# A gated attention and feed-forward stack on one core: GpSimd's large dequantisation operations each in four column pieces

## The reference

```python
x = x + tanh(g_xattn[0]) * L0_xattn(layernorm(x), ctx, mask, ...)      # stage A
x = x + tanh(g_ffn[0])   * L0_ffn(layernorm(x), w_gate, w_up, w_down)  # stage F
x = x + tanh(g_xattn[1]) * L1_xattn(layernorm(x), ctx, ...)            # stage B
x = x + tanh(g_ffn[1])   * L1_ffn(layernorm(x), Wr, W1, W2, W3, ...)   # stages R, M

def fp4_quant_dequant(x):            # blocks of 16 along the last dim
    scale = max(abs(xb)) / 6
    idx = searchsorted(MID, abs(xb / scale))
    return GRID[idx] * sign(xb) * scale

def L0_ffn(x, w_gate, w_up, w_down): # widths 256 -> 704 -> 256
    gate, y = fp4_linear(x, w_gate), fp4_linear(x, w_up)
    return fp4_linear(silu(gate) * y, w_down)
```

## Time and profile before

| | us |
|---|---|
| median of 3 runs (1751.59 to 1757.57) | 1753.04 |
| the profiled execution's own time | 1752.59 |
| its span | 1751.0 |
| TensorE busy | 1444.2 (82%) |
| VectorE busy | 1150.0 (66%) |
| ScalarE busy | 910.7 (52%) |
| GpSimd busy | 595.4 (34%) |
| L565 on 704 columns, 32 times | 53.6 |
| L567 on 704 columns, 32 times | 45.2 |
| L565 on 512 columns, 16 times | 22.8 |
| L567 on 512 columns, 16 times | 31.1 |

### The profile page before, as it was taken

How to read it: one execution, slowest core, us unless ns; L and a number is a source line. 1 busy time by engine, 2 the same in 40 slices (tenths; PEclk the granted TensorE clock), 3 DMA queues, 4 the chain that set the end, 5 groups by cost and what they waited for, 6 DMA issues and landing times.

```text
span 1751.0 us, 36348 instructions
## 1 busy us (share of the span) xinstructions
PE 1444.2 (82%) x12061; PEld 1110.5 (63%) x12062; DVE 1150.0 (66%) x2878; ACT 910.7 (52%) x2701; POOL 595.4 (34%) x704
## 2 busy tenths in 40 slices
PE   2335798898888988898888767199999999999994
PEld 1223565665656665665655444188888888888884
DVE  5657788988889888988888652344444444444442
ACT  1112377677666767677666555144445444455442
POOL 0002233343424433343423320234444334344342
PEclk9556799999999999999999988599999999999997
DMA  5002211222022211222022000554223231132124
GB/s 180 9 0 84 85 35 64 97 97 82 17 97 97 97 37 61 97 97 82 17 88 88 13 7 7 199 180 113 34 32 107 35 105 33 33 105 34 32 30 120
DMA packets 63333, 123.62 MB, mean 71 GB/s; under 512 B 14130, under 2 KB 52140, under 8 KB 59052
## 3 DMA queue, kind: packets, MB, share of 16 engines
q1 hardware_dynamic: 45915, 102.75, 17.0%
q0 software_dynamic: 17312, 19.56, 6.8%
HBM read 78.64 MB, written 48.04 MB: 72 GB/s over the span
## 4 chain that ended last, share of the span: by engine, by line
PE 51%; DVE 28%; ACT 7%; issue 6%; POOL 5%; DMA 1%; SPq 0%; DVEq 0%; ACTq 0%; POOLq 0%
PE bank L1312 13%; PE bank L1314 13%; PE bank L1313 13%; PE bank L1388 3%; DVE b_mn L1047 2%; ACT b_ex L710 2%; POOL f_z L567 2%; PE bank L1401 2%; DVE wm L1125 1%; POOL f_z L565 1%; DVE wm L1117 1%; DVE r_pick L1219 1%; PE bank L1424 1%; DVE a_t L1037 1%; POOL slots L595 1%
## 5 line engine op out<-in xcount | busy, mean ns | idle before, releaser
L1312 PE MATMUL bank<-split_room,wm 128*128 128x256 f16 x1152 | 315.5, 274 | 8.2 <-issue 6.8
L1313 PE MATMUL bank<-split_room,wm 128*128 128x256 f16 x1152 | 315.4, 274 | 0.0
L1314 PE MATMUL bank<-split_room,wm 128*128 128x256 f16 x1152 | 315.3, 274 | 0.0
L1289 DVE SCALAR_TENSOR_TENSOR split_room<-bank,b12e,split_room 128x256 f32<-128x256 f32 x288 | 138.1, 483 | 267.2 <-ACT split_room L833 260.1
L710 ACT ACTIVATE b_ex<-bank,b_mn 128x120 f32<-128x120 f32 x512 | 177.4, 360 | 130.0 <-DVE b_mn L1047 121.1
L833 ACT ACTIVATE split_room<-bank,b12e 128x256 f32<-128x256 f32 x288 | 134.1, 470 | 197.1 <-PE bank L1314 193.7
L656 POOL DMA_INDIRECT acc<-split_room,m_cur x72 | 115.3, 1601 | 132.5 <-ACT split_room L847 105.7
L1314 PE MATMUL bank<-wm,split_room 128*128 128x256 f16 x576 | 157.0, 273 | 0.0
L1313 PE MATMUL bank<-wm,split_room 128*128 128x256 f16 x576 | 157.0, 273 | 0.0
L1312 PE MATMUL bank<-wm,split_room 128*128 128x256 f16 x576 | 157.0, 273 | 0.0
L1388 PE MATMUL bank<-b_k,b_q 128*128 128x480 f32 x256 | 129.1, 586 | 13.9 <-ACT b_q L782 13.9
(11 more groups left out here) (358 smaller groups left out, 3841.8 us busy)
## 6 DMA issues: line engine op xcount, KB each, us to landing
split_room<-in_L_ffn_W SPq DMA_DIRECT2D x48, 512.0 KB, 8.1
wsplit<-split_room SPq DMA_DIRECT2D x16, 1536.0 KB, 6.4
wm<-wsplit SPq DMA_DIRECT2D x16, 1536.0 KB, 8.6
acc<-x SPq DMA_DIRECT2D x17, 256.0 KB, 6.8
xin<-in_x SPq DMA_DIRECT2D x16, 256.0 KB
rows<-r_row SPq DMA_DIRECT2D x16, 256.0 KB, 2.1
ct<-in_ctx SPq DMA_DIRECT2D x16, 120.0 KB
cb<-in_ctx SPq DMA_DIRECT2D x16, 120.0 KB, 5.2
```

Of the source, the lines that this page charges most:

```text
L1289: dve.scalar_tensor_tensor(m_h[:, c % 3], bank[c % 4][:, TILE:2 * TILE], b12e[:, p, 1, c:c + 1], m_s[:, c % 2], ALU.add, ALU.mult).then_in ...
L1312: pe.matmul(o, lh, rh, start=start, stop=False)
L1313: pe.matmul(o, ll, rh, start=False, stop=False)
L1314: return pe.matmul(o, lh, rl, start=False, stop=stop)
```

## The change

Each of the two operations in `dequantise` is issued as four operations on a quarter of the columns, one behind the other with no wait between them: 4 x 176 columns for the hidden tiles, 4 x 128 for the input. Only the last of each four signals its semaphore. The one wait between the subtractions and the multiplications stays, as do all other waits, the stage table and all other engines' instructions. GpSimd has 18 further instructions in a step, 288 over the 16 batch entries.

```diff
--- before.py
+++ after.py
@@ -33,6 +33,7 @@
 SLOTS = NE * REGION + TILE
 FILL = 2.3819763e38
 QUAD = 4
+PIECES = 4
 HL = 33
 VHALF = H1 // 2 * PITCH + K1
 WCH = 6
@@ -562,9 +563,16 @@
             def dequantise(b, n, v, m, scale):
 
                 pool.wait_ge(F.t, b * 3 + n + 1)
-                pool.tensor_tensor(v, v, m, ALU.subtract).then_inc(F.pool, 1)
+                w = v.shape[1] // PIECES
+                cut = [slice(i * w, (i + 1) * w) for i in range(PIECES)]
+                for c in cut:
+                    last = pool.tensor_tensor(v[:, c], v[:, c], m[:, c], ALU.subtract)
+                last.then_inc(F.pool, 1)
                 pool.wait_ge(F.pool, b * 3 + n + 1)
-                pool.tensor_tensor(blocks(v), blocks(v), over(scale, BLK), ALU.mult).then_inc(F.hq, 1)
+                for c in cut:
+                    sc = scale[:, c.start // BLK:c.stop // BLK]
+                    last = pool.tensor_tensor(blocks(v[:, c]), blocks(v[:, c]), over(sc, BLK), ALU.mult)
+                last.then_inc(F.hq, 1)
 
             def f_pt(t):
                 def stage(b, p):
```

## The result

The changed kernel takes 1773.5 us at the median of six runs (1761.4 to 1775.9), the kernel before 1753.7 us in the same comparison. The ratio is 1.0088, with a 95% interval of 1.0069 to 1.0107: slower by 0.9%. (The medians alone are 1.1% apart; the changed kernel's six runs fall into two groups, and the means, 1770.2 and 1754.4 us, are 0.9% apart.) I had forecast 1738 us, faster by 0.9%, with a range up to 1758. The runs also spread by 14 us, where those of before spread by 6. Two of the six took 1761.4 and 1763.0 us, the other four 1773.5 to 1775.9; the profiled execution is the one of 1763.0, with a span of 1761.4.

What follows compares the result with a forecast made beforehand. Bound: a chain alternating between engines, VectorE and TensorE with little time to spare, GpSimd with plenty. 14 x (1.3 + 0.8) - 16 x 0.9 = 15 us gained from 1752.6 us, stated as 1738 us, range 1722 to 1758.

Steps and rivals of the forecast that it cites:

- What a piece costs: Each further GpSimd operation costs 0.15 us; quarters start every 0.52 and 0.44 us, each pair 0.9 us longer.
- Who gets on between two pieces: A waiting VectorE operation goes next, between two GpSimd operations that follow each other without a wait.
- no gap: Rival, chance 0.08: four GpSimd pieces keep VectorE out as one operation does; 38 us lost, 1790 us.
- Place 1: First hidden tile: VectorE's L1219 and L1225 wait for GpSimd; 1.3 us gained in 14 steps, bounds 0.1 and 2.1.
- in step: Rival, chance 0.14: every tiny operation loses a piece, Place 1 gains only 0.1 us; 1755 us, no change.
- the tiny operations: VectorE's L1229 to L1236 at Place 1: can lose one rest of a piece each, two or three times, 0.5 us.
- Place 2: Second hidden tile: VectorE's rotary additions wait for GpSimd; 0.8 us gained in 14 steps, bounds 0.3 and 1.0.
- Place 3: Input tile: TensorE waits for GpSimd's own result; 0.9 us lost, 16 times, bounds 0.6 and 1.1.
- GpSimd too late: Rival, chance 0.10: a piece costs over 0.15 us; gain gone at 0.23 us, 1764 us at 0.30.

Runs made afterwards that it cites:

- late_input: Kernel before, nothing cut, two tiny GpSimd operations behind the input tile's multiplication delaying its signal: 1783.5 us, ratio 1.0178.
- all_filler: Changed kernel plus six matmuls of 512 columns, results thrown away, in TensorE's wait for the input tile: 1737.25 us, ratio 0.9891.
- before_filler: Kernel before plus two useless matmuls of 512 columns in TensorE's wait for the input tile: 1756.25 us, ratio 0.9998.

## Why the prediction was wrong

By its own steps:

- **What a piece costs.** Right. 0.52 and 0.45 us between starts, 0.9 us more for a pair.
- **Who gets on between two pieces.** Right. In each of the three cut places a waiting VectorE operation goes next at a boundary; the rival "no gap" needed `r_pick` to wait for all four.
- **Place 1.** Forecast 1.3 us; 1.27 by the trace, 1.34 by the run that cuts it alone. The rival "in step" did not come about, though three of the tiny operations do wait, as I had said, and lose 0.8 us in place of 0.5.
- **Place 2.** Forecast 0.8 us; 0.9 by the trace, 0.8 by the run that cuts it alone.
- **Place 3.** Here is the step that failed. "TensorE has idled here before, so nothing hides the 0.9 us lost; bounds 0.6 and 1.1." The wait grew by 1.0 us, within the bounds. But I priced a longer wait of TensorE at its own length, with an upper bound from durations alone, and left out what TensorE does after it. In the profiled execution 13 of these waits, of 1.54 to 1.74 us, lie between 250 and 950 us. In eight of them (at 257 and the seven from 592 to 940 us) the clock fell during the wait, and the transposes took 1.12 us and not 0.66. After two more, at 313 and 535, it fell 1.4 and 1.5 us after TensorE had gone on. In the kernel before, with 0.52 to 0.73 us of waiting at this place, it did not fall at any of the 13, and its clock from 195 to 959 us is 1.00 against 0.96. In seven steps TensorE worked at half speed for 6.3 us after the wait, and 3.0 us were lost each time; in the three others the clock came back sooner, and about 1.7 us were lost (the step of 56.7 us is one). 7 x 3.0 + 3 x 1.7 = 26 us from the 1763.0 of this execution leave 1737. So with the clock held up the sum stands: 14 x (1.27 + 0.88) - 16 x 1.0 = 14 us gained by the rows, against the 15 of the forecast. The term that was missing is the clock after the wait. The forecast had it at nothing, without a reason given, and it was 26 us in this execution and some 36 at the median of the runs.
- **The rivals.** All three that I gave were about GpSimd. The harsher half of "GpSimd too late" (1764 us at 0.30 us a piece) lay nearest to the measured time, but by a price that did not come about: no piece cost more than 0.15 us beyond its columns. The rival that was missing could have been read from the trace of the kernel before, though not as a certainty. Two rows of TensorE that I had not looked at:

```profile
622.45 0.65 PE L1401 MATMUL bank<-C,b_ex 128*120 128x128 f32 x4 [2.11 <-ACT b_ex L710]
...
984.20 1.12 PE L1470 MATMUL bank<-C,f_z 128*128 128x128 f32 x4 [2.77 <-POOL f_z L567]
```

The second is place 3 for the last batch entry, where TensorE waited for 2.77 us, and the transposes took 1.12 us: the price was there. The first speaks against it. In 12 steps TensorE waited for 1.58 to 2.11 us at L1401, some 30 us behind place 3, and the clock stayed at 1.00. The 0.99 of the earlier trace rows comes from falls behind 959 us and says nothing of the steady steps. The Trainium skill, "TensorE: Matmul & The Clock Gate", in its first part, says that the engine's clock is gated down when it has been idle and released by activity. The trace agrees with the direction of that at place 3, and not at L1401.

Chain of causes, with what shows each link: the cut makes GpSimd's input pair 1.0 us longer (trace); TensorE's wait grows from 0.6 to 1.6 us (trace); its clock then falls in a part of the steps (trace; and, without any cut, late_input); with the same wait filled, the clock stays up and 36 us come back (all_filler). What is shown is this wait, at this place.

What stays open: why the clock fell at some waits of 1.6 us and not at others. In the profiled execution it stayed at 1.00 through the three steps from 365 to 531 us, and fell in each from 592 to 940, where the steps are 58.0 us long to a tenth. In late_input, waits of 1.55 and 1.56 us went both ways. Nor is the length of the wait enough to tell: at L1401, in the kernel before, 12 waits of 1.58 to 2.11 us passed without a fall, while in before_filler one of 2.06 us at the same line, ending at 622.6, was followed by one. What differs around the two places, or in the timing, no run tested. How often it happens is most likely what makes the changed kernel's runs spread from 1761 to 1776 us; the mean clock recorded for a whole run speaks for it: 0.920 and 0.921 in the two of 1763 and 1761 us, 0.912 or 0.913 in the other four. (A mean that is 0.0075 lower over 1770 us is 13 us of lost full-speed time, and the runs are 11 us apart.) Steps can't be told apart in these, as they have no trace.

## What to carry to other kernels

When an edit makes TensorE wait longer, write down as a rival what half speed for the following microseconds would cost, and look in the trace for longer waits at the same place, with the durations of the matmuls behind them. Here a wait of 0.6 us was harmless and one of 1.6 us was not, while waits as long elsewhere in the step were harmless too. And cut an operation of a helper engine where others wait for it to let go, not where they wait for its result: the same edit gained 30 us in two places and lost 35 us in the third. The rows of before told them apart: at the first two, short VectorE operations ended just after a GpSimd operation did, and at the third TensorE's idle time was ended by GpSimd. And for a delay that can't be avoided, filling the wait with useless matmuls was worth 36 us.

## What the runs showed of the hardware that I had not expected

- In 10 of 13 waits of 1.54 to 1.74 us before the same matmuls, the granted clock fell to its lower level, during the wait or up to 1.5 us after it, and TensorE then worked at half speed for up to 6.3 us. With 0.52 to 0.73 us there it fell in none of 13. Useless matmuls of 1.46 us in the gap, which left 0.31 us of it, prevented it in every steady step. At another place of the step 12 waits of 1.58 to 2.11 us brought no fall.
- Between two GpSimd operations that follow each other without a wait, a VectorE operation that waits for the first gets on. A VectorE operation on 2 columns takes 0.22 us alone and 1.23, 0.68 or 0.31 us beside GpSimd operations on 704, 352 or 176 columns. The products of 256 columns that read PSUM (L1034, L1035 in the kernel before) are not held up: 0.41 us beside an operation on 704 columns.
